# Making the two halves of a weight's low part in two steps of VectorE's loop

## What is computed

```python
def _L0_cond_ref(x, cat_ids, W, b):            # x (128, 128, 512), W (64, 512, 512)
    out = jnp.einsum('bsd,bdh->bsh', x, W[cat_ids]) + b[cat_ids][:, None, :]
    return out

def _L0_ffn_ref(x, weight):
    w_scale = jnp.mean(jnp.abs(weight)) + EPS
    w_quant = jnp.clip(jnp.round(weight / w_scale), -1.0, 1.0)
    a_scale = jnp.max(jnp.abs(x), axis=-1, keepdims=True) + EPS
    a_quant = jnp.round(jnp.clip(x / a_scale * 127.0, -128.0, 127.0))
    y = jnp.einsum('bsi,oi->bso', a_quant, w_quant)
    return y * (w_scale * a_scale / 127.0)

out = x + _L0_ffn_ref(_L0_cond_ref(x, itok, L0_cond_W, L0_cond_b), L0_ffn_weight)
```

## Time and profile before

| | us |
|---|---|
| median of three runs | 546.17 |
| lowest and highest of them | 544.36 and 547.55 |
| the profiled execution, its own time | 543.38 |
| its span in the trace | 541.5 |
| TensorE matmul busy | 512.7 (95%) |
| VectorE busy | 392.5 (72%) |
| ScalarE busy | 343.7 (63%) |
| GpSimd busy | 281.2 (52%) |

### The profile page before, as it was taken

One profiled execution on the slowest core, in us unless ns is written; L12 is line 12 of the kernel. 1 busy time (PEld: TensorE's weight loads), 2 busy tenths in 40 slices (PEclk: granted clock), 3 DMA queues, 4 the chain that ended last, 5 costly groups with the idle time before them and its releaser, 6 DMA issues.

```text
span 541.5 us, 13855 instructions
## 1 busy us (share of the span) xinstructions
PE 512.7 (95%) x2584; PEld 355.8 (66%) x2585; DVE 392.5 (72%) x652; ACT 343.7 (63%) x502; POOL 281.2 (52%) x396
## 2 busy tenths in 40 slices
PE   4799999999999999999999998999989999999996
PEld 1576667666776666677676665667657677777774
DVE  3787765879667968966866858776797868758763
ACT  3577565765676567666756666766766666666753
POOL 3695455444556364555554463555446455565540
PEclk9999999999999999999999999999999999999999
DMA  5899879998899999979989889987999999899963
GB/s 170 276 404 351 291 258 310 382 364 274 324 364 343 367 333 392 356 243 372 350 291 294 325 322 398 365 288 271 407 332 363 329 363 342 273 310 333 323 194 117
DMA packets 71728, 172.76 MB, mean 319 GB/s; under 512 B 8096, under 2 KB 8224, under 8 KB 64800
## 3 DMA queue, kind: packets, MB, share of 16 engines
q1 hardware_dynamic: 71712, 172.59, 90.0%
HBM read 139.00 MB, written 33.55 MB: 319 GB/s over the span
## 4 chain that ended last, share of the span: by engine, by line
PE 35%; DVE 6%; issue 5%; DVEq 2%; ACT 2%; DMA 2%; ACTq 0%; SPq 0%; POOL 0%; POOLq 0%
PE ps_cond L619 9%; PE ps_cond L621 8%; PE ps_cond L620 8%; PE ps_y L587 8%; DVE sb_w_lo L486 3%; PE ps_aT L597 2%; DVE sb_absmax L527 2%; DMA sb_bias<-cond_b 2%; DVEq L165 1%; ACT sb_a_rounded L406 1%; ACT sb_w_hi L355 1%; DVE sb_a_step L530 0%; ACTq L165 0%; DVE sb_x_rows L520 0%; DVEq L486 0%
## 5 line engine op out<-in xcount | busy, mean ns | idle before, releaser
L619 PE MATMUL ps_cond<-sb_w_hi,sb_xT_hi 128*128 x512 | 220.7, 431 | 6.7 <-issue 3.2
L621 PE MATMUL ps_cond<-sb_w_hi,sb_xT_lo 128*128 x512 | 200.3, 391 | 0.0
L620 PE MATMUL ps_cond<-sb_w_lo,sb_xT_hi 128*128 x512 | 199.4, 389 | 0.0
L486 DVE TENSOR_TENSOR sb_w_lo<-sb_w_raw,sb_w_hi x106 | 162.1, 1567 | 20.2 <-issue 16.8
L317 POOL TENSOR_TENSOR sb_xT_lo<-sb_xT_raw,sb_xT_hi 128x512 fp32r<-128x512 f32 x128 | 166.4, 1300 | 10.9
L527 DVE TENSOR_REDUCE sb_absmax<-ps_cond 128x1 f32<-128x512 f32 x128 | 87.7, 686 | 100.6 <-PE ps_cond L621 89.1
L406 ACT ACTIVATE sb_a_rounded<-ps_cond,sb_rounder,sb_a_inv 128x512 f32<-128x512 f32 x128 | 99.5, 777 | 94.9 <-DVE sb_a_inv L533 94.5
L334 POOL TENSOR_SCALAR sb_y_scale<-sb_absmax,sb_w_step 128x1 f32<-128x1 f32 x128 | 41.0, 320 | 224.6 <-DVE sb_absmax L527 224.3
L587 PE MATMUL ps_y<-sb_ffnT,sb_aT 128*128 128x512 bf16 x512 | 131.2, 379 | 1.6 <-DVE sb_ffnT L512 0.9
L619 PEld LDWEIGHTS ps_cond<-sb_w_hi,sb_xT_hi 128*128 128x128 f32 x512 | 96.2, 188 | 51.7 <-issue 27.2
L396 ACT ACTIVATE sb_aT<-ps_aT 128x512 bf16<-128x512 int16 x128 | 75.4, 589 | 67.5 <-PE ps_aT L597 62.8
(11 more groups left out here) (69 smaller groups left out, 36.2 us busy)
## 6 DMA issues: line engine op xcount, KB each, us to landing
sb_w_raw<-cond_w SPq DMA_DIRECT2D x53, 1024.0 KB, 6.6
sb_xT_raw<-x_t SPq DMA_DIRECT2D x128, 256.0 KB, 5.1
sb_x_rows<-x SPq DMA_DIRECT2D x128, 256.0 KB, 5.2
out<-sb_x_rows SPq DMA_DIRECT2D x128, 256.0 KB, 4.9
sb_bias<-cond_b SPq DMA_DIRECT2D x54, 256.0 KB, 7.9
sb_ffn_raw<-ffn_t SPq DMA_DIRECT2D x1, 1024.0 KB, 6.9
sb_w_raw<-cond_w SPq DMA_DIRECT2D x4, 256.0 KB, 6.7
sb_cat_row_i<-itok SPq DMA_DIRECT2D x1, 64.0 KB, 3.5
```

The lines of the kernel that those rows point to most:

```text
L486: dve.tensor_tensor(w_lo[:, bass.ds(at, PIECE)], w_raw[:, bass.ds(at, PIECE)], w_hi[:, bass.ds(at, PIECE)].bitcast(F32), ALU.subtract).the ...
L619: pe.matmul(ps_cond, x_hi_k, w_hi_k, start=False, stop=False, skip_group_check=True)
L620: pe.matmul(ps_cond, x_hi_k, w_lo_k, start=False, stop=False, skip_group_check=True)
L621: last_mm = pe.matmul(ps_cond, x_lo_k, w_hi_k, start=False, stop=(k == KD - 1), skip_group_check=True)
```

## The change

`split_low` makes one half instead of two. VectorE's body r now calls it twice: for the second half (piece 1) of step r+2, and then for the first half (piece 0) of step r+3. Each call loads the table's two values anew and has its own branch and its own `Else`, which waits for the count of halves so far and adds one. The loop ahead of the bodies makes three calls instead of two (both halves of step 1, the first of step 2). The order of the halves is the same as before; the second half of every weight is made one body later.

```diff
-            def split_low(new, offset, step):
+            def split_low(new, offset, step, piece):
                 with dve.If(new > 0):
-                    for piece in range(PIECES):
-                        at = offset + piece * PIECE
-                        dve.wait_ge(w_hi_done, (step - 1) * PIECES + piece + 1)
-                        dve.tensor_tensor(w_lo[:, bass.ds(at, PIECE)], w_raw[:, bass.ds(at, PIECE)],
-                                          w_hi[:, bass.ds(at, PIECE)].bitcast(F32), ALU.subtract).then_inc(w_lo_done, 1)
+                    at = offset + piece * PIECE
+                    dve.wait_ge(w_hi_done, (step - 1) * PIECES + piece + 1)
+                    dve.tensor_tensor(w_lo[:, bass.ds(at, PIECE)], w_raw[:, bass.ds(at, PIECE)],
+                                      w_hi[:, bass.ds(at, PIECE)].bitcast(F32), ALU.subtract).then_inc(w_lo_done, 1)
                 with dve.Else():
 
-                    if type(step) is not int or step > 1:
-                        dve.wait_ge(w_lo_done, (step - 1) * PIECES)
-                    dve.sem_inc(w_lo_done, PIECES)
+                    if type(step) is not int or (step - 1) * PIECES + piece > 0:
+                        dve.wait_ge(w_lo_done, (step - 1) * PIECES + piece)
+                    dve.sem_inc(w_lo_done, 1)
 
             dve.wait_ge(table_done, 1)
             for step in range(1, LO_AHEAD):
                 new, offset = w_slot(dve, step)
-                split_low(new, offset, step)
+                for piece in range(PIECES):
+                    if step * PIECES + piece < (LO_AHEAD - 1) * PIECES + 1:
+                        split_low(new, offset, step, piece)
...
+
+                if not last or u + LO_AHEAD - 1 < U:
+                    new, offset = w_slot(dve, r + LO_AHEAD - 1)
+                    split_low(new, offset, r + LO_AHEAD - 1, 1)
                 if not last or u + LO_AHEAD < U:
                     new, offset = w_slot(dve, r + LO_AHEAD)
-                    split_low(new, offset, r + LO_AHEAD)
+                    split_low(new, offset, r + LO_AHEAD, 0)
```

## The result

The changed kernel is slower: 567.6 us (median of four, 566.3 to 568.8) against 545.8, a ratio of 1.040 with a 95% interval of 1.037 to 1.042. That is 22 us, where the prediction had 36 above the profiled execution of the kernel before (579 in a range of 558 to 600). The profiled execution took 568.8 us, its span 567.0.

A forecast was written before the change was run, and what follows sets the result against it. VectorE, its sequencer included, was taken to decide the time, not the busier TensorE. Body 2 at 27.9, 125 bodies' 539.7, 2 of waiting, a 7.5 tail and 1.9 around the span gave 579 us against 543.4; range 558 to 600.

The forecast's parts named there:

- What bounds the kernel before: VectorE's time per body, late where consecutive steps make new low parts; about 20 of TensorE's 26 us held up.
- The second block: Extra table load, branch and Else on VectorE's sequencer, nothing to hide under: 1.10 us, plus 0.15 per load that shows.
- neither: VectorE body that makes no half, for step r+2 or r+3: 3.6 us, 36 of 125 bodies.
- behind a run: VectorE body that makes only the second half of r+2, held by GpSimd, then an Else: 4.35 us, 36 bodies.
- First of a run: VectorE body with an Else for r+2, then the first half of r+3, free of GpSimd: 4.58 us, 36 bodies.
- inside: VectorE body new at both r+2 and r+3, making two halves: 5.21 us as now, 17 bodies.
- The late weights: SyncE's weight loads issued later in 25 places, ScalarE's a_rounded 0.6 us late: priced at 0, at most 15 us.
- The views named beforehand: Signs in the profile: waits of maxima and matmuls, times of dense and sparse bodies, VectorE's busy time hardly moving.
- The hidden block: Rival: VectorE's sequencer runs the added block under the data path; 547 us, chance 0.08.
- spreading as the winner: Rival: block hidden and VectorE's halves free of GpSimd, most of the 20 us go; 524 us, chance 0.05.
- The rival of the late weights: Rival: late weights cost 15 us (594), slower table loads 24 on top, given as 603; chance 0.07 beyond 598.
- The instruction fetches: Rival: VectorE's longer loop, some 133 to 173 instructions, is refetched each pass, 29 us; 608 us, chance 0.04.

The follow-up runs named there:

- before_short_xlo: The kernel before with GpSimd's low part of x made for 64 of 512 columns, the rest zero: 527.5 us, ratio 0.968.
- two_blocks: The kernel before with each half in a block of its own, both halves still in one body: 563.7 us, ratio 1.034.
- the late load alone: The kernel before with SyncE waiting for one more low half ahead of a weight's load, VectorE's program untouched: 554.9 us, ratio 1.018.
- two_blocks_late: The kernel before with two blocks, both halves in one body, and the weight's load a body later: 569.6 us, ratio 1.044.
- pool_early: The kernel before with GpSimd starting on x when the first product is done, not right behind the maxima: 532.3 us, ratio 0.974.

## Why the prediction was right, and where it was off

**What bounds the kernel before** stood. Runs of new steps make VectorE late, TensorE forgives 1.65 us of it, and some 20 us go: taking the cause away (`before_short_xlo`) gave back 18.

**The second block** was the right mechanism, shown alone by `two_blocks`, but its term was too large. I had a body of kind "neither" at 3.6 us (2.15 + 1.10 + 2 x 0.15). In the 19 of these bodies in which the block holds the next maxima it takes 3.37 on average in the changed kernel. The kernel before has no such body of this kind; its 16 bodies behind a run that end so take 2.41, with the same work in them. A block thus costs 0.96 and not 1.25. One part of that shows in the rows of table loads. Only 126 of 253 blocks need the register operation that I had counted at 0.1 each (112 of 127 did before):

```profile
L165 DVEq TENSOR_LOAD <-sb_table x253: 521/528/2206, 17.3 to 552.9; - x127
...
L165 DVEq FUSED_REGOPS  x126: 69/69/75, 52.9 to 529.9; - x126
```

36 such bodies at 0.23 are 8 us, of which TensorE took 3 back: in the other 17 bodies VectorE waits for it, and the 36 took 5 us more than 36 x 3.37, where I had 2.

**The halves.** First of a run 4.51 against 4.58, inside 5.33 against 5.21, behind 4.26 against 4.35: in sum 406.1 against 410.1. These sums hold whatever the late weights cost in them too. The half behind the second block runs free of GpSimd (1.23 at 180.03) in 31 of 36 bodies, and the one behind a run is held (2.23 at 194.65) in 31 of 36. Halves of over 1.3 us are 53 of 106, the number that I had named.

**The start.** A third block ahead of the bodies was priced at 1.1; the first maxima came at 19.63 and not 18.95, and at body 2 only 0.3 were left (27.16 and 26.82). The tail is 567.0 - 559.5 = 7.5, as predicted. Together these terms are the 10 us between a span of 577 and one of 567.

**The late weights** are the step that failed. I worked out that ScalarE would be some 0.6 us late in 25 places and that TensorE could not pass this on, and set the price to 0, at most 15. The load goes out where I said and ScalarE waits 40 us where I had 25 x 1.5 = 38; but it is not free. Alone it costs 9.5 us, on top of the block 5.5. For ScalarE's own path the reasoning nearly held: with the late load alone TensorE stood ahead of its transposes 2 us longer. What the step left out is TensorE's own table load. Slow loads were in the sum for VectorE only; with the weights sent later it is TensorE's that become slow, and it stood ahead of its first product 7 us longer. This path is read from the profiles and was not tried by an experiment.

That the forecast missed by 11 us only, and not by more, is partly luck: a block priced too high and late weights priced at nothing run against each other. Neither error alone would have left the range.

**The views named beforehand.** The dense bodies 38 to 51 took 242.05 - 177.05 = 65.0 us (64 predicted), the sparse 110 to 122 52.9 (55). VectorE's busy time moved by 5 us, as said. Three of the waits did not come as named: the maxima's waits for TensorE fell to 35.6 us and not under 15; their waits for the block rose to 35.7 us and not to 60, since in the bodies that open a run the block shows as idle time ahead of the half (the 1.20 of body 38; 52 us in these 36 bodies, against 15 before) and not of the maxima; and the matmuls' wait for `a_rounded` rose from 9.7 to 12.8, with that of their weight loads from 21.5 to 33.3, 15 in all and not 25.

**The rivals.** The hidden block is out (3.18 us for a late body with nothing to make), and so is spreading as the winner: `two_blocks_late` puts its gain at 2 us. The rival of the late weights was added up wrongly: 594 and 24 are 618; 603 is the 579 with slow loads alone. The instruction fetches stayed at 17 packets (q8 5, q14 12) for the longer loop: no refetch.

## What to carry to other kernels

Splitting an optional piece of work over two steps doubles its bookkeeping in every step, the idle ones too; price the table load, branch and `Else` at their sequencer time and ask what hides them, since busy time will not show them. When a step is moved later, follow who frees a buffer by it: the transfer behind it moves too, and it can cost a good part of what the edit itself does. Then ask by which path, engine by engine: the longest new wait (ScalarE's 40 us) was hardly felt by TensorE. A view of waits puts an idle time down to what ended last; check that the engine named was really needed there. When one instruction takes twice its usual time in some bodies only, look at what a neighbour that shares its port does just then, and move the neighbour.

## What the runs showed of the hardware

A block of one table load, one branch and a semaphore costs 0.96 us of VectorE's time when nothing hides it, with a load of 0.53 us in the median and up to 2.2.

A table load that starts 2.8 to 4.0 us behind the issue of a 1 MB weight's transfer takes about 1.1 us in the mean and not 0.6 (VectorE's in the kernel before, 25 and 97 loads; TensorE's with the late load, 28 and 95). In the other profiles the two engines' means are 0.7 to 1.2 us in that window and 0.6 to 0.7 outside. What makes such a load slow is not shown.

VectorE's subtraction of two SBUF operands and GpSimd's exclude each other both ways: VectorE's took 2.2 us and not 1.22 behind GpSimd, and GpSimd's took 2.14 and not 1.3 behind VectorE's. The Trainium skill's lock ("SBUF — State Buffer", section "SBUF: two separate sides") is what these rows show. VectorE's maxima from PSUM took 0.68 to 0.69 us also in `pool_early`, where GpSimd works beside nearly all of them, which is what makes moving GpSimd under them pay.
